# Edge counting over stretches of 64, 256 and 1024 columns, and the second adjacency transposition placed beside it

## The reference

```python
M = Bc * Nc                                    # 5120
loops = jnp.arange(M, dtype=edge_index.dtype)
src = jnp.concatenate([edge_index[0], loops])
dst = jnp.concatenate([edge_index[1], loops])
...
e = jax.nn.leaky_relu(a_src[src] + a_dst[dst], negative_slope=0.2)
e_max = jax.ops.segment_max(e, dst, num_segments=M)
ee = jnp.exp(e - e_max[dst])
denom = jax.ops.segment_sum(ee, dst, num_segments=M)
alpha = ee / (denom[dst] + 1e-16)
msg = h[src] * alpha[:, :, None]
agg = jax.ops.segment_sum(msg, dst, num_segments=M)
```

## Time and profile before

| what | value |
|---|---|
| median of three runs | 4091.95 us |
| the profiled execution's own time | 4086.21 us |
| its span in the trace | 4084.5 us |
| TensorE matmul busy, share of the span | 3276.6 us, 80% |
| VectorE busy | 2596.1 us, 64% |
| ScalarE busy | 1305.9 us, 32% |
| GpSimd busy | 125.9 us, 3% |

### The profile page before, as it was taken

How to read it: one execution, slowest core, us unless ns; L and a number is a source line. 1 busy time by engine, 2 the same in 40 slices (tenths; PEclk the granted TensorE clock), 3 DMA queues, 4 the chain that set the end, 5 groups by cost and what they waited for, 6 DMA issues and landing times. The chain is left out here.

```text
span 4084.5 us, 58633 instructions
## 1 busy us (share of the span) xinstructions
PE 3276.6 (80%) x22169; PEld 2093.0 (51%) x22169; DVE 2596.1 (64%) x4477; ACT 1305.9 (32%) x2440; POOL 125.9 (3%) x163
## 2 busy tenths in 40 slices
PE   5278999999999996246549996588885988995998
PEld 5234555555555553145426665355553666763665
DVE  6536777676776766598643343699995346873333
ACT  2223333333333332000434452211112433443444
POOL 0000000000000000000000000022220000000000
PEclk7688999999999998655769996799997977887999
DMA  3211111211112111100013211000001200001232
GB/s 36 87 37 35 48 35 35 55 35 48 35 35 55 35 42 25 50 0 0 27 49 75 67 39 15 1 0 0 0 0 31 71 24 1 2 1 49 65 77 65
DMA packets 139573, 141.54 MB, mean 35 GB/s; under 512 B 63764, under 2 KB 121520, under 8 KB 136904
## 3 DMA queue, kind: packets, MB, share of 16 engines
q1 hardware_dynamic: 139376, 138.68, 14.1%
HBM read 130.64 MB, written 8.01 MB: 34 GB/s over the span
## 5 line engine op out<-in xcount | busy, mean ns | idle before, releaser
L801 DVE TENSOR_TENSOR f_hg<-f_hs,f_gb 128x640 f32<-128x640 f32 x320 | 263.8, 825 | 507.4 <-ACT f_hs L783 447.9
L2132 PE MATMUL hy_ps<-hy_uT,hy_win 128*128 128x512 f32 x1152 | 498.7, 593 | 0.0
L783 ACT ACTIVATE f_hs<-f_ph,f_b1t 128x320 f32<-128x320 f32 x640 | 334.9, 527 | 405.7 <-PE f_ph L751 402.5
L751 PE MATMUL f_ph<-XNP,f_w 128*128 (+1 forms) x1280 | 403.5, 439 | 12.8 <-PEq L641 8.6
L766 PE MATMUL f_po<-f_hg,f_w 128*128 128x320 f32 x1280 | 404.4, 439 | 10.9 <-DVE f_hg L801 10.9
L2132 PEld LDWEIGHTS hy_ps<-hy_uT,hy_win 128*128 128x128 f32 x1152 | 217.6, 190 | 281.3 <-issue 281.3
L751 PEld LDWEIGHTS f_ph<-XNP,f_w 128*128 128x128 f32 x1280 | 247.0, 193 | 117.3 <-issue 18.3
L766 PEld LDWEIGHTS f_po<-f_hg,f_w 128*128 128x128 f32 x1280 | 240.2, 191 | 127.7 <-issue 20.9
L1660 PE MATMUL er_c<-XNG 128*128 128x400 f32 x544 | 210.6, 528 | 48.1 <-POOL XNG L1591 48.1
L2192 PE MATMUL hy_ps<-hy_wo,hy_yg 128*128 128x512 f32 x512 | 229.1, 606 | 0.0
L1605 ACT ACTIVATE er_OT<-er_t 128x384 bf16<-128x384 f32 x128 | 61.0, 489 | 346.6 <-PE er_t L1630 346.6
(11 more groups left out here) (497 smaller groups left out, 5732.8 us busy)
## 6 DMA issues: line engine op xcount, KB each, us to landing
f_gb<-gate_rows SPq DMA_DIRECT2D x32, 1280.0 KB, 8.5
XNG<-hy_decays SPq DMA_DIRECT2D x32, 1024.0 KB, 9.4
hy_rb<-hy_inverse SPq DMA_DIRECT2D x128, 128.0 KB, 3.2
f_gb<-gate_rows SPq DMA_DIRECT2D x16, 640.0 KB, 5.2
hy_xn<-XNP SPq DMA_DIRECT2D x1, 4096.0 KB, 12.5
hy_XC<-hy_xn SPq DMA_DIRECT2D x16, 256.0 KB, 3.2
XNG<-in_L_ffn_edge_index_dram SPq DMA_DIRECT2D x2, 2048.0 KB
xin<-in_x_dram SPq DMA_DIRECT2D x5, 512.0 KB, 6.7
```

Source lines behind the costliest of these rows:

```text
L751: pe.matmul(psh[e % 2][k][:], w1[:, e, k * 128:(k + 1) * 128], chunk_view(g, c), start=True, stop=True).then_inc(h_ps, 1)
L783: ins = act.activation(hs[:, e % 2, k, :], psh[e % 2][k][:], ACT.Gelu, bias=b1t[:, e * H2 + k:e * H2 + k + 1])
L801: dve.tensor_tensor(hg[:, e % 2], hs[:, e % 2], gb[:, par, e, None, :].broadcast_to([128, H2, CH]), ALU.mult).then_inc(hg_ready, 1)
L2132: mm = pe.matmul(p[:], win[:, t, m * 128:(m + 1) * 128], uT[:, t, :], start=(t == 0), stop=(t == KT - 1))
```

## The change

The change touches the two stages.

1. **Masks and keys.** Six fused VectorE instructions, a COPY and a product take the place of the list of simple ones. The mask is made directly as 0 or -1, and the count of kept edges is taken from it by ScalarE (ACT) with an accumulating copy instead of by a VectorE reduction. Keys are now (target + 1) x 1024 + the position in a stretch of 1,024 columns; GpSimd makes a table `place` of 1,024 positions for this.
2. **Extraction in three widths.** First each of 64 stretches of 64 columns gives up its 8 largest keys once, then each of 16 stretches of 256 columns, once. The 640 keys so found are spelled out in 40 pieces in straight-line code. What is left is taken by the loop, now from 4 stretches of 1,024 columns, 32 keys and 2 pieces a round. The number of rounds comes from the count of what is left.
3. **The adjacency turned alongside.** The stage `turn_adjacency` of the second graph layer is gone. In `edge_keys` GpSimd sets `adjT` to zero, TensorE does the 128 transposes first thing, and ScalarE, which had no work in this stage, copies them out.

```diff
-        SEG, LO, HI = 128, 128, T // 128
-        SEGS = EC // SEG
-        KC = SEGS * GRP
+        HG, LO, HI = 16, 128, T // 128
+        FINE, MID, WIDE = 64, 256, 1024
+        KF, KM, KW = (EC // n * GRP for n in (FINE, MID, WIDE))
+        KS = KF + KM
...
         @block.gpsimd
+            pool.iota(place[:], pattern=[[-1, WIDE]], base=-WIDE, channel_multiplier=0, allow_small_or_imprecise_dtypes=True).then_inc(io, 1)
             pool.memset(g.ones[:], 1.0)
             pool.memset(zero[:], 0.0).then_inc(zeroed, 1)
+            pool.memset(g.adjT[:], 0.0).then_inc(cleared, 1)
+
+        @block.scalar
+        def _(act):
+            act.wait_ge(cleared, 1)
+            for c in range(NCH):
+                act.wait_ge(at_ps, c + 1)
+                for j in range(2):
+                    ins = act.activation(g.adjT[rows(j), c * CHP:(c + 1) * CHP, j, :], psa[c % 2][j][rows(j), :, :], ACT.Copy)
+                ins.then_inc(at_out, 1)
+                if c == NCH // 2:
+                    act.wait_ge(masked, 1)
+                    act.activation(spent, mask[:], ACT.Copy, scale=-1.0, accum_out=cnt[:, 0:1]).then_inc(summed, 1)
...
         @block.vector
-            dve.tensor_scalar(w, dst, 13, VALID, ALU.logical_shift_left, ALU.bitwise_or)
-            dve.tensor_scalar(past, src, float(T - 1), None, ALU.is_ge)
-            dve.tensor_scalar(keep, dst, float(T), None, ALU.is_lt)
-            dve.drain()
-            dve.tensor_tensor(w, w, src, ALU.bitwise_or)
-            dve.tensor_tensor(past, past, keep, ALU.mult)
...
+            dve.tensor_scalar(keys, dst, float(T), -1.0, ALU.is_lt, ALU.mult)
+            dve.scalar_tensor_tensor(w, dst, 13, src, ALU.logical_shift_left, ALU.bitwise_or)
+            dve.drain()
+            dve.scalar_tensor_tensor(mask[:], src, float(T - 1), keys, ALU.is_lt, ALU.mult)
+            dve.scalar_tensor_tensor(past, src, float(T - 1), keys, ALU.is_ge, ALU.mult)
+            dve.drain()
+            dve.nop().then_inc(masked, 1)
+            dve.scalar_tensor_tensor(w, w, VALID, mask[:], ALU.bitwise_or, ALU.bitwise_and)
+            dve.wait_ge(io, 1)
+            dve.scalar_tensor_tensor(keys.rearrange("p (s c) -> p s c", c=WIDE), dst.rearrange("p (s c) -> p s c", c=WIDE), float(-WIDE),
+                                     place[:, None, :].broadcast_to([128, EC // WIDE, WIDE]), ALU.mult, ALU.add)
+            dve.tensor_copy(spelled[:], iob[:, 0:LO, None].broadcast_to([128, LO, HG]))
+            dve.drain()
+            dve.tensor_tensor(keys, keys, past, ALU.mult)
+            dve.drain()
+
+            def extract(width, base):
+                part = lambda i: keys[:, i * width:(i + 1) * width]
+                found = lambda i: K[:, base + i * GRP:base + (i + 1) * GRP]
+                for i in range(EC // width):
+                    dve.max(found(i), part(i))
+                dve.drain()
+                for i in range(EC // width):
+                    dve.match_replace(part(i), found(i), part(i), 0.0)
...
+            extract(FINE, 0)
+            dve.drain()
+            extract(MID, KF)
+            dve.drain()
+            dve.tensor_scalar(past, keys, 0.0, None, ALU.is_gt)
+            digits(slice(0, KS))
+            dve.tensor_reduce(seg[:], past.rearrange("p (s c) -> p s c", c=WIDE), AX.X, ALU.add)
+            dve.drain()
             dve.tensor_reduce(cnt[:, 1:2], seg[:], AX.X, ALU.max)
             dve.drain()
             dve.nop().then_inc(counted, 1)
...
+            for c in range(KS // HG):
+                one_hot(c, c % 2, c * HG)
             dve.wait_ge(c_ps, 1)
             dve.tensor_reduce(top[:], pc[:], AX.X, ALU.max)
...
+            n = dve.value_load(g.turns[0:1, 1:2], min_val=1, max_val=WIDE // GRP)
             with dve.Fori(0, n) as r:
+                extract(WIDE, KS)
+                dve.drain()
+                digits(slice(KS, KS + KW))
+                for c in range(KW // HG):
+                    one_hot(KS // HG + r * (KW // HG) + c, c % 2, KS + c * HG)
...
         @block.tensor
+            pe.wait_ge(adjacency.loaded, 32)
+            for c in range(NCH):
+                if c >= 2:
+                    pe.wait_ge(at_out, c - 1)
+                for q in range(CHP):
+                    for j in range(2):
+                        mm = pe.matmul(psa[c % 2][j][rows(j), q, :], g.adjG[rows(j), c * CHP + q, :], g.ident[rows(j), rows(j)], start=True, stop=True)
+                mm.then_inc(at_ps, 1)
+            pe.wait_ge(zeroed, 1)
+            pe.matmul(ph[:], zero[:, 0:LO], zero[:, 0:HI], start=True, stop=False, skip_group_check=True).then_inc(h_ps, 2)
+            pe.wait_ge(summed, 1)
             pe.wait_ge(counted, 1)
...
+            for c in range(KS // HG):
+                counts(c, c % 2)
             pe.wait_ge(sized, 1)
```

More of the change, by code:

```diff
@@ L99, in load, with turn_adjacency @@
             sp.dma_start(g.adjG[rows(j), :, :], pairs[j]).then_inc(self.loaded, 16)
-def turn_adjacency(nc, g, name, adjacency, blocks):
+def turn_adjacency(nc, g, name, adjacency):
     with nc.cleanup_on_exit(), ExitStack() as ctx:
@@ L115, in _ @@
             pool.wait_ge(steps, 1)
[L116 to L125, removed]
+            for j in range(2):
+                o = blk[SLOT * j:SLOT * j + SLOT, :].rearrange("p (a c) -> p a c", c=10)
+                pool.affine_select(out=o, in_=o, compare_op=ALU.is_ge, fill=0.0, base=0,
+                                   pattern=[[-10, 4], [0, 10]], channel_multiplier=1).then_inc(steps, 1)
+                pool.wait_ge(steps, 2 + 2 * j)
+                pool.affine_select(out=o, in_=o, compare_op=ALU.is_ge, fill=0.0, base=9,
+                                   pattern=[[10, 4], [0, 10]], channel_multiplier=-1).then_inc(steps, 1)
+                pool.wait_ge(steps, 3 + 2 * j)
             pool.nop().then_inc(blk_ready, 1)
@@ new lines, in one_hot @@
+            def one_hot(c, b, at):
+                cols = slice(at, at + HG)
+                dve.wait_ge(h_ps, c + 1)
+                dve.tensor_tensor(OL[:, b], spelled[:], dl[:, None, cols].broadcast_to([128, LO, HG]), ALU.is_equal)
+                dve.tensor_tensor(OH[:, b], spelled[:, 0:HI], dh[:, None, cols].broadcast_to([128, HI, HG]), ALU.is_equal).then_inc(hot, 1)
+            extract(FINE, 0)
[3 more added lines that the diff above has]
+            dve.tensor_scalar(past, keys, 0.0, None, ALU.is_gt)
@@ L2520, in graph_network @@
             load_x(nc, g, xin, adjacency)
-            turn_adjacency(nc, g, "a0", adjacency, True)
+            turn_adjacency(nc, g, "a0", adjacency)
             layer_norm(nc, g, True, "n0", tok=xin)
@@ L2531, in graph_network @@
         adjacency = Adjacency(nc, ctx, g, "a1")
-        edge_keys(nc, g, adjacency)
         with nc.sbuf_tensor("adjT1", [128, PAIRS, 2, N], F32) as adjT:
             g.adjT = adjT
-            turn_adjacency(nc, g, "a1", adjacency, False)
+            edge_keys(nc, g, adjacency)
             layer_norm(nc, g, True, "n2")
```

86 lines of the change are left out of this document (33 added, 53 removed).

## The result

The changed kernel takes 4030.72 us (median of 4 runs, 4025.95 to 4039.10); the kernel before takes 4091.03 us in its 4 runs. The ratio is 0.9861, with a 95% interval of 0.9841 to 0.9881, so 49 to 65 us less. The forecast was 4033.5 us. The profiled execution took 4031.54 us, its span 4029.8 us.

A forecast was written before the change was run, and what follows sets the result against it. The prediction took VectorE's instruction list as the bound. 40.2 us off edge_keys plus 18.2 us for the adjacency's stage made 58.4 us, taken from the median 4091.95 us to give 4033.5 us; range 4022 to 4044.

The forecast's parts named there:

- The bound: Both touched stages: VectorE's list is the chain, 25.27 of 25.66 us busy a round, TensorE a close second.
- The preparation: Masks and keys after the edges land: new VectorE list takes 30.0 us, 20.1 us less than before.
- the two bounds of the fused integer instructions: Five fused mask and key instructions: 2.21 us or 4.42 us each; the latter taken, the former 10.9 us less.
- The extraction gains nothing: MAX8 and replace passes in three widths: 61.2 us against 58.9 us before, so 2.3 us more.
- Rival C: 64-column MAX8 passes: a floor makes them cost what 128 columns do, 29.4 instead of 20.9 us, total 4042 us; 5%.
- Three rounds: Loop over stretches of 1,024: the fullest has 17 past edges left by count on the inputs, so 3 rounds.
- rival E: Loop: more than three rounds, each further one costing 14.4 us, so four give 4047.9 us; 1%.
- The price of a round: One loop round: extraction 9.5, splitting 1.7 and two pieces 3.15 us.
- Cover of the adjacency: Adjacency turned inside edge_keys: hidden behind VectorE, ScalarE done near 1710 us with 47 us slack, 18.2 us saved.
- rival B: Adjacency in edge_keys: not covered, transposes at the head of TensorE's queue delay pieces, total 4051.7 us; 3%.
- rival A: Long run of 40 pieces: TensorE's clock rises, a piece costs 1.54 us, 2.9 us less, total 4030.6 us; 5%.
- rival D: Pieces before the loop: TensorE waits for its written-out instructions; at 3.3 us a piece the total is 4101 us; 2%.

The follow-up runs named there:

- a1: Kernel before, with only the adjacency zeroed, turned and copied inside edge_keys and its own stage gone; 4070.06 us, ratio 0.9969.
- a2: Changed kernel, with the adjacency turned in its own stage again; 4044.64 us, ratio 0.9903 to the kernel before.
- b3: Changed kernel, with one-hot tables split as 64 x 80 instead of 128 x 40; 4058.87 us, ratio 0.9932 to the kernel before.
- c1: Changed kernel, with matmuls of 128 weight columns and 80 moving columns instead of 40, 40 of them zero; 4068.38 us.
- c2: Changed kernel, with only 64 of the 128 table columns as weights and 40 moving columns, half the targets uncounted; 4042.17 us.
- a4: Changed kernel, with 8 instead of 16 matmuls a piece, so half of the found keys are not counted; 4034.71 us.
- b2: Changed kernel, with three buffers of one-hot tables in the 40 pieces before the loop; 4031.83 us.
- a5: Changed kernel, with one loop round more than needed, which finds only zeros; 4040.68 us.

## Why the prediction was right, step by step

| term | predicted, us | measured, us |
|---|---|---|
| preparation | 30.0 | 30.09 |
| 64 stretches of 64 | 20.9 | 20.86 (1713.79 to 1734.65) |
| 16 stretches of 256 | 11.8 | 11.88 (to 1746.53) |
| comparison | 2.2 | 2.20 (to 1748.73) |
| splitting 640 keys | 4.0 | 3.64 (to 1752.37) |
| reduction and count | 4.7 | 4.77 (to 1757.14) |
| 40 pieces | 64.3 | 64.37 (to 1821.51) |
| count to the loop | 2.15 | 2.15 (to 1823.66) |
| three rounds | 43.0 | 42.73 (to 1866.39, with the forecast's 0.40 for the last table) |
| wait, copy, memset | 10.5 | 10.46 (to 1876.85) |
| the adjacency's stage | -18.2 | -18.1 (a1), -18.3 (a2) |

- **The bound.** That VectorE's list is the chain held in every kernel but b3, c1 and c2, in which TensorE was made slower. The second half of the step, that TensorE is a close second, was read from its busy time, 22.41 of 25.66 us, and that reading was wrong: TensorE's 16 loads take 1.32 us of 1.61 and it waits for VectorE in every piece. What a4 and b2 took back, 0.07 us a piece, is the delay of one piece through two buffers. The sum did not suffer, because it used the distance of 1.608 us, in which the wait is contained.
- **The preparation.** The choice between the two bounds of the fused integer instructions was right: all five are 4.42 us long, and the 10.9 us of a faster form did not come.
- **The extraction gains nothing.** 61.2 us were forecast; 20.86 + 11.88 and three times (4.68 + 4.94) are 61.6 us. The slope of 1.044 ns a column, from rows at 128 and 4,096 columns, gave the 64-column MAX8 to 4 ns: 64 of them take 8.20 us, 128 ns each, where 132 were put. Rival C is out.
- **Three rounds.** The count on the inputs held, rival E is out. The price of a round, 14.35 us, was 0.8% high against the three rounds (14.24 us each) and 1.5% high against a5. The splitting of 32 keys takes 1.54 us, not 1.7, and the two pieces 3.08 us, not 3.15, since the second does not wait; extraction, 9.62 us and not 9.5, takes part of that back. Both splittings were priced from the first round's 2.53 us, while the second round of the kernel before took 2.33 us (1793.35 to 1795.68); that was the term most in error, 0.36 us for the 640 keys.
- **Cover of the adjacency.** Forecast done near 1710 us, measured 1708.0. a1 and a2 show the full 18 us, rival B is out.
- **The clock, rival A.** The granted clock is 0.50, so 1.2 GHz, in the whole run of pieces, 65.44 us with TensorE busy 60.01, though TensorE pauses in each piece. It does rise elsewhere in the program: from 1640 to 1670 us of the same execution the mean is 0.83. In c1 TensorE is busy without a gap for 85 us, and the clock is still 0.50:

```profile
1765.00:1850.00 85.00, 85.00 (x558) 81.96 (x557) 56.28 (x70) 0.00 (x0) 0.00 (x0) 0.50 0.00 1
```

  So the rule of the Trainium skill that sustained activity releases the throttle ("TensorE: Matmul & The Clock Gate", Part 1) does not hold for this work. What activity it is that would count, no run here shows. b2 took rival A's 2.9 us by a third buffer instead. Rival A's 4030.6 us is nearer to the measured 4030.72 than the forecast, but that is chance: neither the clock nor the distance of the pieces moved.
- **Straight-line code, rival D.** 640 matmuls written out run at 1.61 us a piece, as the loop did. Rival D is out.
- **The total.** 58.8 us from the two stages in the trace, 60.3 us by the medians, 58.4 us forecast. The forecast's only free choice, to start from the median of three runs and not from the profiled execution, was worth 5.7 us, more than all errors of the terms together. That the two times agree to 2.8 us is in part luck: the terms account for 0.4 us of it and the new median of the kernel before for 0.9, and the four runs of the changed kernel alone span 13 us.

## What to carry to other kernels

When one engine's list is the whole chain of a stage, start-to-start distances and a slope from two widths price a rewrite of that list to a per cent. Find whole small stages whose work fits beside such a chain on idle engines, and check only who is queued behind it. With extraction by MAX8, compare what a pass costs with how many keys it finds: two cheap full passes more before the loop can save far dearer rounds in it. And do not take an engine's busy share for its pace: look at what its instructions wait for, and at the distance of their starts.

## What the hardware showed that I had not expected

- A bf16 weight load of 64 columns takes longer (218 ns in c2) than one of 128 columns (149 ns in the changed kernel), both with 40 moving columns at clock 0.50, and the matmuls come 120 instead of 83 ns apart.
- TensorE at 100% busy with 128x80 bf16 matmuls (c1) stayed at the lower clock level for 85 us.
- ScalarE's accumulating activations over 1,024 columns take 1044 ns and their read of the accumulator another 0.2 us; an accumulating copy over 4,096 int32 columns took 3.62 us.
